# Adding transfers that alternate between two tables, with the two tables summed at the end

## The reference

```python
x = x + layernorm(attention(layernorm(x)))        # 16 query heads, 4 key heads, rope, causal
x = x + layernorm(ffn(layernorm(x)))
# ffn(v): aff = sigmoid(v @ wa); p, i = top_k(aff, 2); p = p / sum(p)
#   expert e: y = (gelu(v @ g[e] + gb[e]) * (v @ w1[e] + b1[e])) @ w2[e] + b2[e]
#   ffn(v) = v + sum of 2 shared experts + sum over the 2 chosen of 16 routed experts of p * y
```

## Time and profile before

| | |
|---|---|
| median of 3 runs | 2240.34 us (2237.93 to 2244.18) |
| the profiled execution | 2243.7 us, span 2242.0 us |
| TensorE busy | 1819.2 us, 81% |
| VectorE busy | 869.6 us, 39% |
| ScalarE busy | 581.5 us, 26% |
| GpSimd busy | 439.8 us, 20% |
| mean granted TensorE clock | 0.882 |
| chain that ended last | PE 48%, DMA 22%, DVE 16%, issue 5%, ACT 5%, POOL 2% |
| of it, the adding transfer into `Z` | 19% |

### The profile page before, as it was taken

One profiled execution on the slowest core, in us unless ns is written; L12 is line 12 of the kernel. 1 busy time (PEld: TensorE's weight loads), 2 busy tenths in 40 slices (PEclk: granted clock), 3 DMA queues, 4 the chain that ended last, 5 costly groups with the idle time before them and its releaser, 6 DMA issues.

```text
span 2242.0 us, 23891 instructions
## 1 busy us (share of the span) xinstructions
PE 1819.2 (81%) x7806; PEld 1045.2 (47%) x7807; DVE 869.6 (39%) x2031; ACT 581.5 (26%) x1151; POOL 439.8 (20%) x637
## 2 busy tenths in 40 slices
PE   4488888888888888886569999997988889888970
PEld 3354555555544555543346666664433334333430
DVE  2545455564656455563434222211221212222227
ACT  2133233343434233344221111111211112111113
POOL 1022121222222121221102111111111112111223
PEclk8588889888989889897779999998998989999995
DMA  3535343435544353433124444443455544554437
GB/s 112 64 70 85 78 122 89 123 91 113 128 100 108 76 122 72 123 85 132 61 83 160 151 153 148 155 151 132 122 140 162 141 118 92 140 117 116 98 50 304
DMA packets 116113, 262.80 MB, mean 117 GB/s; under 512 B 15084, under 2 KB 40686, under 8 KB 110136
## 3 DMA queue, kind: packets, MB, share of 16 engines
q1 hardware_dynamic: 99496, 223.65, 35.7%
q0 software_dynamic: 16496, 37.63, 8.5%
HBM read 240.11 MB, written 109.08 MB: 156 GB/s over the span
## 4 chain that ended last, share of the span: by engine, by line
PE 48%; DMA 22%; DVE 16%; issue 5%; ACT 5%; POOL 2%; SPq 1%; DVEq 0%; POOLq 0%; ACTq 0%
PE bank L1732 25%; DMA z_scratch<-wst,idx 19%; PE bank L1836 4%; PE bank L1813 4%; PE bank L1839 3%; PE bank L1796 3%; DVE wst L1580 2%; DVE tmp L1222 2%; DVE hb L1574 1%; PE bank L1923 1%; ACT P L1040 1%; PE bank L1919 1%; PE bank L1899 1%; DVE rp L1230 1%; PE bank L1798 1%
## 5 line engine op out<-in xcount | busy, mean ns | idle before, releaser
L1290 DVE TENSOR_REDUCE mx<-bank 128x1 f32<-128x512 f32 (+3 forms) x352 | 219.5, 634 | 209.1 <-PE bank L1798 208.2
L1040 ACT ACTIVATE P<-bank 128x512 f32<-128x512 f32 x320 | 190.3, 595 | 411.6 <-PE bank L1813 410.5
L1941 PE MATMUL bank<-ring,xg 128*128 x632 | 287.5, 598 | 0.0
L1710 POOL DMA_INDIRECT z_scratch<-wst,idx x79 | 122.7, 1553 | 515.3 <-DVE wst L1580 504.0
L1796 PE MATMUL bank<-Ks,Qs 96*128 96x384 f32 (+3 forms) x512 | 167.6, 394 | 68.8 <-DVE mx L1290 36.8
L1732 PE MATMUL bank<-ws,xt 128*128 128x512 f32 x768 | 197.5, 406 | 12.7 <-DMA xt<-xt_scratch 12.7
L1813 PE MATMUL bank<-Qs,Ks 97*128 97x512 f32 x320 | 162.1, 507 | 42.9 <-ACT P L1040 36.9
L1558 DVE COPY wcol<-xs 128x1 f32<-128x1 f32 x79 | 12.1, 154 | 456.6 <-DMA z_scratch<-wst,idx 443.1
L1732 PEld LDWEIGHTS bank<-ws,xt 128*128 128x128 f32 x768 | 141.9, 191 | 73.3 <-issue 31.4
L1941 PEld LDWEIGHTS bank<-ring,xg 128*128 128x128 f32 x632 | 116.4, 195 | 115.6 <-issue 115.6
L1958 PE MATMUL bank<-ring,hr 128*128 x316 | 169.2, 664 | 0.0
(11 more groups left out here) (229 smaller groups left out, 2573.1 us busy)
## 6 DMA issues: line engine op xcount, KB each, us to landing
ring<-in_w SPq DMA_DIRECT2D x79, 1024.0 KB
ring<-in_w SPq DMA_DIRECT2D x79, 512.0 KB
Qs<-st SPq DMA_DIRECT2D x192, 128.0 KB, 4.7
xs<-xs_scratch SPq DMA_DIRECT2D x79, 258.0 KB, 2.7
xs_scratch<-xs_scratch SPq DMA_DIRECT2D x78, 258.0 KB, 4.9
xt<-xt_scratch SPq DMA_DIRECT2D x32, 512.0 KB, 3.2
xs<-xn_scratch SPq DMA_DIRECT2D x64, 256.0 KB, 2.8
xt_scratch<-xt SPq DMA_DIRECT2D x30, 512.0 KB, 4.8
```

Of the source, the lines that this page charges most:

```text
L1040: e.activation(Pt[:, p, :], bank[PA.bank[step]][:, :], ACT.Exp, scale=SCALE).then_inc(s_exp, 1)
L1290: e.tensor_reduce(mx[:, G % 2, :].rearrange("p (h i) -> p h i", i=4)[:, h:h + n, i:i + 1], bank[PA.bank["max", b, p, j]][:, 0:n * k].rearr ...
L1710: e.indirect_dma_start(Z, bass.IndirectOffsetOnAxis(ap=idx[:, s:s + 1], axis=0), yo[:, o, :], None, compute_op=ALU.add).then_inc(d_ys[o], 16)
L1941: e.matmul(ps[:, :].rearrange("p (o n) -> p o n", o=1), xg[:, q, 128 * k:128 * k + 128], ring[:, bass.ds(reg[n], 1), 512 * k:512 * k + 512 ...
```

## The change

Odd adding transfers go to `XN` (the normalised rows) and even ones to `Z`, which now holds the shared sums without the normalised rows. `XN` gets 128 padding rows. GpSimd's wait before transfer n is for transfer n-2. At the end both tables are loaded, and VectorE adds two tiles and GpSimd the other two tiles of each group. The final buffers `zf` and `zx` lie in one region `zall` that covers the weight ring and the staging buffers; `zx` has room for 4 groups, so loads of group g+4 wait for the sums of group g.

```diff
-    XN = nc.dram_tensor("xn_scratch", [NT, 128, D], F32, kind="Internal").ap()
+    XN = nc.dram_tensor("xn_scratch", [NT * 128 + 128, D], F32, kind="Internal").ap()
+            zall = nc.alloc_sbuf_tensor_at("zall", [128, NT + 16, 512], F32, offset=low)
-        zf = ring[:, :, :].rearrange("p a b -> p (a b)")[:, 0:NT * 512].rearrange("p (t d) -> p t d", t=NT)
+        zf, zx = zall[:, 0:NT, :], zall[:, NT:NT + 16, :]
+        tables = (Z, XN)
...
@@ SP, shared experts
                     if n == 0:
-                        e.dma_start(Z[NT * 128:NT * 128 + 128, :], zs[:, 0, :]).then_inc(d_zs[0], 16)
+                        for v in tables:
+                            e.dma_start(rows_of(v, NT), zs[:, 0, :]).then_inc(d_zs[0], 16)
@@ SP, final stretch
+            def fetch(g):
+                if g < NG:
+                    if g >= 4:
+                        w.wait_ge(f_sum, 2 * (g - 3))
+                        w.wait_ge(f_psum, 2 * (g - 3))
+                    e.dma_start(group(zf, g), Z_g[g]).then_inc(d_zg[g % 4], 16)
+                    e.dma_start(group(zx, g % 4), XN_g[g]).then_inc(d_zg[g % 4], 16)
+            for g in range(4):
+                fetch(g)
             for g in range(NG):
-                e.dma_start(group(zf, g), Z_g[g]).then_inc(d_zg[g], 16)
-            for g in range(NG):
+                fetch(g + 4)
                 for h in range(2):
@@ VectorE, last "down" of a tile
                     if t >= 3:
-                        w.wait_ge(d_zs[t % 3], 16 * (t // 3 + (t % 3 == 0)))
-                    e.tensor_tensor(zs[:, t % 3, :], bank[PM.bank[step]][:, :], xs[:, s, 0, 0:512], ALU.add).then_inc(zs_dve, 1)
+                        w.wait_ge(d_zs[t % 3], 16 * (t // 3 + 2 * (t % 3 == 0)))
+                    e.tensor_copy(zs[:, t % 3, :], bank[PM.bank[step]][:, :]).then_inc(zs_dve, 1)
@@ VectorE, final stretch
-                w.wait_ge(d_zg[g], 16)
-                for t in range(4 * g, 4 * g + 4):
+                w.wait_ge(d_zg[g % 4], 32 * (g // 4 + 1))
+                for i in range(2):
+                    e.tensor_tensor(zf[:, 4 * g + i, :], zf[:, 4 * g + i, :], zx[:, 4 * (g % 4) + i, :], ALU.add).then_inc(f_sum, 1)
+                for i in range(4):
+                    w.wait_ge(f_sum if i < 2 else f_psum, 2 * g + 1 + i % 2)
+                    t = 4 * g + i
                     e.bn_stats(bst3[:, t, :], zf[:, t, :]).then_inc(dve_own, chain.up())
@@ GpSimd, adding transfer n
-                    if n:
-                        w.wait_ge(d_ys[(n - 1) % 3], 16 * ((n - 1) // 3 + 1))
+                    if n >= 2:
+                        w.wait_ge(d_ys[(n - 2) % 3], 16 * ((n - 2) // 3 + 1))
+                    elif n:
+                        for i in range(2):
+                            w.wait_ge(d_xs[i], 16 * NT)
-                    e.indirect_dma_start(Z, bass.IndirectOffsetOnAxis(ap=idx[:, s:s + 1], axis=0), yo[:, o, :], None,
+                    e.indirect_dma_start(tables[n % 2], bass.IndirectOffsetOnAxis(ap=idx[:, s:s + 1], axis=0), yo[:, o, :], None,
                                          compute_op=ALU.add).then_inc(d_ys[o], 16)
@@ GpSimd, final stretch
+            def add(g):
+                if g < NG:
+                    w.wait_ge(d_zg[g % 4], 32 * (g // 4 + 1))
+                    for i in range(2, 4):
+                        e.tensor_tensor(zf[:, 4 * g + i, :], zf[:, 4 * g + i, :], zx[:, 4 * (g % 4) + i, :], ALU.add).then_inc(f_psum, 1)
+            add(0)
             for g in range(NG):
+                add(g + 1)
```

More of the change, by code:

```diff
@@ L477, in program, with rows_of @@
     Z = nc.dram_tensor("z_scratch", [NT * 128 + 128, D], F32, kind="Internal").ap()
+    def rows_of(v, t):
+        return v[128 * t:128 * t + 128, :]
     x_t = x.rearrange("b (i p) d -> (b i) p d", p=128)
@@ L638, in program @@
         zs = wst[:, 1536:3072].rearrange("p (a b) -> p a b", a=3)
-        zf = ring[:, :, :].rearrange("p a b -> p (a b)")[:, 0:NT * 512].rearrange("p (t d) -> p t d", t=NT)
-        Z_g = Z[0:NT * 128, :].rearrange("(g p i) d -> g p (i d)", g=NG, p=128)
+        zf, zx = zall[:, 0:NT, :], zall[:, NT:NT + 16, :]
+        tables = (Z, XN)
+        Z_g, XN_g = (v[0:NT * 128, :].rearrange("(g p i) d -> g p (i d)", g=NG, p=128) for v in tables)
         X1_g = X1.rearrange("t p d -> (t p) d").rearrange("(g p i) d -> g p (i d)", g=NG, p=128)
@@ L660, in program @@
         rturn_pe, hr_act, rdown_pe, yo_dve = sem("rturn_pe"), sem("hr_act"), sem("rdown_pe"), sem("yo_dve")
-        d_zg, d_o = sems("d_zg", NG), sem("d_o")
-        f_mean, f_rs, f_x1, f_out = sem("f_mean"), sem("f_rs"), sem("f_x1"), sem("f_out")
+        d_zg, d_o = sems("d_zg", 4), sem("d_o")
+        f_sum, f_psum, f_mean, f_rs, f_x1, f_out = sem("f_sum"), sem("f_psum"), sem("f_mean"), sem("f_rs"), sem("f_x1"), sem("f_out")
         read_by = {"xT": (xT_lo, "xTlo"), "max": (max_dve, "max"), "maxT": (mT_act, "mTcp"), "rb": (yn_dve, "ynm"),
@@ L838, in _ @@
                     w.wait_ge(xn_act, nth("xn", (b, i)))
-                    e.dma_start(XN[4 * b + i], xn[:, :]).then_inc(d_s2[R], 16)
+                    e.dma_start(rows_of(XN, 4 * b + i), xn[:, :]).then_inc(d_s2[R], 16)
                     if b < B - 1 and i < 3:
@@ L895, in load_rows @@
                     for n in range(2):
-                        e.dma_start(xs[:, s, n, 0:512], XN[t]).then_inc(d_xs[s], 16)
+                        e.dma_start(xs[:, s, n, 0:512], rows_of(XN, t)).then_inc(d_xs[s], 16)
             load(0)
@@ L936, in _ @@
                     if n == 0:
-                        e.dma_start(Z[NT * 128:NT * 128 + 128, :], zs[:, 0, :]).then_inc(d_zs[0], 16)
-                    e.dma_start(Z[128 * n:128 * n + 128, :], zs[:, n % 3, :]).then_inc(d_zs[n % 3], 16)
+                        for v in tables:
+                            e.dma_start(rows_of(v, NT), zs[:, 0, :]).then_inc(d_zs[0], 16)
+                    e.dma_start(rows_of(Z, n), zs[:, n % 3, :]).then_inc(d_zs[n % 3], 16)
                     load_rows(n + 2)
@@ L1704, in _ @@
                     w.wait_ge(idx_dve, n + 1)
-                    if n:
-                        w.wait_ge(d_ys[(n - 1) % 3], 16 * ((n - 1) // 3 + 1))
+                    if n >= 2:
[3 more added lines that the diff above has]
+                            w.wait_ge(d_xs[i], 16 * NT)
                     else:
                         for i in range(3):
-                            w.wait_ge(d_zs[i], 16 * (len(range(i, NT, 3)) + (i == 0)))
-                    e.indirect_dma_start(Z, bass.IndirectOffsetOnAxis(ap=idx[:, s:s + 1], axis=0), yo[:, o, :], None,
+                            w.wait_ge(d_zs[i], 16 * (len(range(i, NT, 3)) + 2 * (i == 0)))
+                    e.indirect_dma_start(tables[n % 2], bass.IndirectOffsetOnAxis(ap=idx[:, s:s + 1], axis=0), yo[:, o, :], None,
                                          compute_op=ALU.add).then_inc(d_ys[o], 16)
+            def add(g):
[4 more added lines that the diff above has]
+            add(0)
             for g in range(NG):
+                add(g + 1)
                 c_ = slice(4 * g, 4 * g + 4)
```

## The result

| | before | after |
|---|---|---|
| median | 2240.34 us (5 runs, 2237.93 to 2244.58) | 2255.21 us (5 runs, 2252.01 to 2257.81) |
| ratio | | 1.0061, 95% interval 1.0045 to 1.0078 |
| profiled execution's span | 2242.0 us | 2256.1 us |

The change makes the kernel slower by about 0.6%. A second measurement of the same kernel on another occasion gave 1.0049 (1.0036 to 1.0062), so 0.5 to 0.6%. The forecast was 2248.4 us with a range of 2241 to 2261, and slower as the likeliest direction. Difference of the spans: 14.1 us.

A forecast was written before the change was run, and what follows sets the result against it. VectorE's wait in "take" for transfer n-4 was taken to hold the loop at 7.1 us a round. Terms: -8.2 + 2.5 + 9.9 + 1.5 + 2.4 = +8.1 us, giving 2248.4 us, range 2241 to 2261.

The forecast's parts named there:

- lock rival: Final stretch: each group GpSimd's first add wins against VectorE's add, 9.4 us in place of 2.4, 2255.4 us; chance 0.17.
- The loop, 0 us: Adding transfers 1 to 75: the removed GpSimd wait was already satisfied, VectorE's wait for landings stays; gain 0.
- The last three transfers, -8.2 us: Transfers 76 to 78, not behind VectorE's wait in "take", leave earlier and overlap; gain 8.2 us.
- The rival without overlap: Loop's end: two adding transfers take turns, so 8.2 us are not gained, 2256.6 us; chance 0.11.
- The first load, +2.5: Start of the final stretch: group 0 needs two loads of 1.05 MB, not one; +2.5 us.
- VectorE's adds, +9.9: Final stretch: VectorE adds 16 tiles from SBUF at 0.62 us each; +9.9 us.
- Waits of the first groups, +1.5: Start of the final stretch: 0.8 us until group 1 lands and 0.7 for the statistics; +1.5 us.
- Collisions with GpSimd, +2.4: Final stretch: GpSimd's SBUF adds delay VectorE's two-input instructions by 0.3 us in each of 8 groups; +2.4 us.
- The shared experts, 0: Before the routed experts: 32 adds become copies and a 256 KB store is added, hidden behind waits for TensorE; 0.
- The transfers as the pace of the end, 0.12: Rival, final stretch: loads and stores at 347 GB/s set the pace, +12.9 us in all, 2253.2 us; chance 0.12.

## Why the prediction was right

The measured 2255.2 us lies in the stated range of 2241 to 2261, on the side that was called likeliest. The central forecast of 2248.4 was too low, and its own range of 2243 to 2254 just misses: +8.1 us were forecast, +14.1 measured between the two traces (+14.9 between the medians). The parts show what was right and what was not. That the lock rival's 2255.4 us meets the measured time is luck: it had 9.4 us of collisions, and 4.7 were found.

*The loop, 0 us.* Right: 590.4 before, 589.8 after, and the landing at 4.8 us in the median on both. The agreement to 0.6 us is in part luck, since three other traces with alternation and 4 columns have 594.5 to 595.8. The experiments with 8 columns show the reason given, VectorE's wait in "take"; the one with transfers on one table shows that the removed wait was worth only the last three.

*The last three transfers, -8.2 us.* Measured -7.95. Transfer 76 left 2.36 us behind 75, as worked out, and landed in 4.76 us, about the median of all. The rival without overlap, 2256.6 us, is near the measured time, but for a reason that did not occur.

*The first load, +2.5.* Measured 2192.90 - 2185.45 = 7.45 us to the first add, against 4.97: +2.5.

*VectorE's adds, +9.9.* 16 at 1.20 / 2 us: 9.7.

*Waits of the first groups, +1.5.* 0.52 and 1.46 us, less the 0.37 that the first products waited before: +1.6.

*Collisions with GpSimd, +2.4.* Too small. Two pairs of adds took 2.36 in place of 1.28, +2.2; six groups of products took 3.84, 2.62, 2.70, 2.62, 3.11 and 3.37 in place of 2.62, +2.5: 4.7 us. This is the mis-sized term. I had reasoned that GpSimd's adds fall beside VectorE's statistics; they do in the middle groups, but in the first ones both engines wait for the same load and start together, and in two late ones GpSimd waits 0.36 and 0.63 us for a load, so that its adds run on into VectorE's products. The sign named for the rival "lock", records over 1 us, did come: two adds and one product of 1.75 us and products of 1.20 and 1.46. It had the mechanism right, but not in each group: at 9.4 us it was too dear. The rule that the prediction weighed, the Trainium skill's page "SBUF — State Buffer", section "Who interferes with whom", agrees with this trace for VectorE as the loser too: 0.68 us became up to 1.75, 1.07 us more, where a GpSimd add takes 1.26 us alone.

Those terms make 2.5 + 9.7 + 1.6 + 4.7 = 18.5 us, measured 18.35, and with -7.95 a net of +10.4, 2.3 more than forecast.

*The shared experts, 0, and the rest, +3.7.* The first adding transfer leaves 4.3 us later than in the trace of before, and the loop gives 0.6 back. Of the 4.3 us, 2.2 are not the change's: the first product of the shared experts comes that much later, ahead of them, and varies from trace to trace as told above. The other 2.1 us lie between that product and the first adding transfer, 429.0 us against 426.9. In six of the seven traces with the change this stretch takes 428.4 to 429.0 us (425.1 in the seventh, the one without the sums), in the four without it 425.5 to 426.9. So some 2 us are likely the change's, where I had put 0. The copies save nothing: they take 692 ns, as the adds did, and not a few hundredths less. The added 256 KB store may be a part. The one wait of VectorE for `xs` near it is 10.4 to 11.3 us long in the seven traces with that store and 9.5 to 10.7 in the four without, so up to some 1 us may be its price; that was not tried by itself, and the cause of the 2 us stays open.

*The transfers as the pace of the end, 0.12.* It did not come about, but was near: windows with a DMA share of 1.00 or more move 378 to 425 GB/s in the kernel after, and the floor is 64 us under the 70.6. That the fall to 347 GB/s before came with VectorE's pace was right: with stores mixed in, the kernel without the sums still moves 402 to 412. My forecast's own figure for the transfers, 59 us, left out the first landing and the last store.

## What to carry to other kernels

Before a wait is moved, look at who else waits for the same event: here the engine that feeds the transfer waited for its landing 75 times, and one more column of indices gave 4.9% where a second table gave minus 0.6%. A profile tells this in one view, the releaser and the number of times: 3 of 79 waits were the one that the change attacks. And VectorE adds with two SBUF inputs collided with GpSimd's adds first of all where one load released both engines, so count collisions at the places where both wait for one event, not by the mean.

## What was unexpected in the hardware

Two adding transfers in flight to different tables slowed each other little, if at all. In the kernel after, transfers 76 to 78 each left with the one before still in flight and landed in 4.58 to 4.76 us; one at a time they took 4.41 to 4.70. With two tables and 8 columns, 19 transfers left so: 13 landed in 4.7 to 5.1 us, one in 5.7, and five in 7.4 to 8.7. Three of those five are slow in the kernel before too; the other two (17 and 25) are not, and whether the overlap slowed them is open. And with TensorE busy throughout, its granted clock stayed at 1.00 from 1590 to 2060 us, the upper of its levels, while in the kernels before and after, with gaps, it was 0.94 from 1590 to 2160 us; the round of 6.38 us is TensorE's at that level.
